# Attention and FFN on one core: weighted sums alternate between two banks, GpSimd's low halves stand ahead of its additions, and the next tile's normalisation and cast move to other engines

## The reference

```python
xn = _layernorm(x)                                    # x: 8 x 1024 x 128
Q = einsum('bnd,hdk->bhnk', xn, proj_q)               # 8 heads
K = einsum('bmd,dk->bmk', xn, proj_k)                 # one key and one value head
V = einsum('bmd,dv->bmv', xn, proj_v)
weights = softmax(einsum('bhnk,bmk->bhnm', Q, K), axis=-1)
O = einsum('bhnm,bmv->bhnv', weights, V)
Y = einsum('bhnv,hdv->bnd', O, proj_o)
mid = einsum('amh,ehn->aemn', xn, w1)                 # 8 experts, no activation
ffn = einsum('aemn,enh->amh', mid, w2)
return x + Y + ffn
```

## Time and profile before

| what | value |
|---|---|
| median of 3 runs | 1693.48 us (1692.24 to 1694.28) |
| profiled execution, its own time | 1692.57 us |
| its span, first to last instruction | 1690.8 us |
| granted TensorE clock, mean | 0.999 |
| busy: PE, PEld | 1655.1 us (98%), 1212.9 us (72%) |
| busy: DVE, ACT, POOL | 1281.2 us (76%), 1294.1 us (77%), 1335.8 us (79%) |
| matmuls, low halves on GpSimd | 18820, 512 |

### The profile page before, as it was taken

One profiled execution on the slowest core, in us unless ns is written; L12 is line 12 of the kernel. 1 busy time (PEld: TensorE's weight loads), 2 busy tenths in 40 slices (PEclk: granted clock), 3 DMA queues, 4 the chain that ended last, 5 costly groups with the idle time before them and its releaser, 6 DMA issues. The chain is left out here.

```text
span 1690.8 us, 46211 instructions
## 1 busy us (share of the span) xinstructions
PE 1655.1 (98%) x18820; PEld 1212.9 (72%) x18820; DVE 1281.2 (76%) x2761; ACT 1294.1 (77%) x1296; POOL 1335.8 (79%) x956
## 2 busy tenths in 40 slices
PE   7999999999999999999999999999999999999997
PEld 6777777777777777777777777777777777777774
DVE  5777777777777777777777777777777777777774
ACT  4777777777777777777777777777777777877874
POOL 2687888788788788878878878887887888788785
PEclk9999999999999999999999999999999999999999
DMA  7000000000000000000000000000000000000000
GB/s 227 2 2 2 2 2 14 2 2 2 8 8 2 1 2 8 8 2 2 2 8 8 2 1 2 8 8 2 2 2 14 2 2 2 2 14 2 2 2 13
DMA packets 16175, 16.71 MB, mean 10 GB/s; under 512 B 416, under 2 KB 12192, under 8 KB 15968
## 3 DMA queue, kind: packets, MB, share of 16 engines
q1 hardware_dynamic: 14928, 13.24, 2.7%
q10 hardware_dynamic: 1040, 0.52, 0.1%
HBM read 9.57 MB, written 4.19 MB: 8 GB/s over the span
## 5 line engine op out<-in xcount | busy, mean ns | idle before, releaser
L281 POOL TENSOR_TENSOR pr_lo<-pr,pr_hi 128x1024 f16<-128x1024 f32 x512 | 1087.7, 2135 | 328.5 <-ACT pr_hi L364 328.5
L357 ACT ACTIVATE pr<-s_ps,boost,scale 128x1024 f32<-128x1024 f32 x512 | 616.9, 1205 | 241.3 <-PE s_ps L514 222.4
L729 DVE TENSOR_REDUCE key_max<-s_ps 128x128 f16<-128x1024 f32 x512 | 625.7, 1222 | 0.1
L364 ACT ACTIVATE pr_hi<-pr 128x1024 f16<-128x1024 f32 x512 | 525.4, 1051 | 8.1
L512 PE MATMUL s_ps<-g_lo,xT 128*128 128x128 f16 x4096 | 512.9, 219 | 2.1 <-DVE g_lo L742 1.0
L514 PE MATMUL s_ps<-g_hi,xT 128*128 128x128 f16 x4096 | 512.3, 219 | 0.0
L512 PEld LDWEIGHTS s_ps<-g_lo,xT 128*128 128x128 f16 x4096 | 399.3, 98 | 41.7 <-DVE g_lo L742 11.1
L514 PEld LDWEIGHTS s_ps<-g_hi,xT 128*128 128x128 f16 x4096 | 400.8, 98 | 29.9
L398 PE MATMUL t_ps<-pr_hi,xn_hi 128*128 128x512 f16 x1024 | 388.3, 379 | 16.9 <-POOL pr_lo L281 3.2
L400 PE MATMUL t_ps<-pr_hi,xn_lo 128*128 128x512 f16 x1024 | 388.4, 379 | 0.0
L399 PE MATMUL t_ps<-pr_lo,xn_hi 128*128 128x512 f16 x1024 | 388.4, 379 | 0.0
(11 more groups left out here) (117 smaller groups left out, 1548.0 us busy)
## 6 DMA issues: line engine op xcount, KB each, us to landing
out_dram<-xacc SPq DMA_DIRECT2D x16, 256.0 KB, 2.3
w_sb<-in_L_ffn_w_dram SPq DMA_DIRECT2D x1, 2048.0 KB, 10.0
pr<-in_L_attn_proj_q_dram ACTq DMA_DIRECT2D x1, 512.0 KB, 4.4
xacc<-in_L_attn_x_dram SPq DMA_DIRECT2D x2, 256.0 KB, 4.9
pr<-in_L_attn_proj_o_dram SPq DMA_DIRECT2D x1, 512.0 KB, 6.3
xacc<-in_L_attn_x_dram SPq DMA_DIRECT2D x1, 128.0 KB, 6.2
wkv<-in_L_attn_proj_k_dram SPq DMA_DIRECT2D x1, 64.0 KB, 2.7
wkv<-in_L_attn_proj_v_dram SPq DMA_DIRECT2D x1, 64.0 KB, 4.2
```

The costliest lines, as they stand in the source:

```text
L281: pool.tensor_tensor(pr_lo[:, u % RING, :], pr32[:, u % PR, :], pr_hi[:, u % RING, :], ALU.subtract)\
L357: act.activation(pr32[:, u % PR, :], both_banks(u), ACT.Exp, bias=boost[:, 0:1], scale=scale[:, 0:1])\
L364: act.activation(pr_hi[:, u % RING, :], pr32[:, u % PR, :], ACT.Copy).then_inc(p_hi_ready, 1)
L729: dve.tensor_reduce(key_max[:, u % 2, :], both_banks(u).rearrange("p (t q) -> p q t", q=P), AX_X, ALU.max).then_inc(keys_max, 1)
```

## The change

- PSUM: `t_ps` is two banks, and block k's sum lies in bank k % 2 (`sum_bank`). `turn_ps` is gone: the transposed maxima and the row lie in the bank that no sum is using; in period 2 of a block the transposed maxima lie in the scores bank of the next high pass's second half.
- The sum's tiles are spread two to a period (before 3, 2, 2, 1), and tile 0 of the next block starts at the end of period 2: its first product before the transpose of the key maxima, the other two behind it.
- In period 3 the row of maxima follows the high products at once, and VectorE writes it before it reduces the keys.
- GpSimd: `p_low` comes first in each period; the additions of heads move back by one period. VectorE subtracts the last unit's low half and does the last addition.
- The next tile's normalisation moves from VectorE to GpSimd, its cast from VectorE to ScalarE, and their places in the pair change.
- `head_out(k, 1)` and `scale_head(k, 1)` go behind the FFN and the transposed tile. The load of x is cut once more, with tiles 10 to 15 ahead of w2.

The diff's pieces stand in this order: PSUM and its helpers; GpSimd; ScalarE's cast; TensorE's `high_pass`, `weigh` and its loop; VectorE's loop and its end.

```diff
-        t_ps = pb("t_ps", [P, BANK])
-        turn_ps = pb("turn_ps", [P, BANK])
+        t_ps = pb("t_ps", [P, 2 * BANK])
...
+        def summing(n):
+            return (n + 1) // 4 - 2
+        def sum_bank(k):
+            return t_ps[:, (k % 2) * BANK:(k % 2 + 1) * BANK]
+        def turn_bank(n):
+            return sum_bank(summing(n) + 1)
+        def maxima_turned(u):
+            if u % 4 == 2:
+                return bank(u + 1, 1)[:, 0:P // 2].bitcast(F16)
+            return turn_bank(u)[:, 0:P // 2].bitcast(F16)
+        def maxima_row(u):
+            return turn_bank(u + 1)[:, 2 * P:3 * P]
...
+            def normalise_next(tile):
+                pool.wait_ge(ln_rstd, tile + 1)
+                pool.wait_ge(ln_hi, tile)
+                pool.wait_ge(xn_ready, tile)
+                pool.tensor_scalar(xn32[:, 0, 1:D], xacc[:, tile, 1:D], mean_var[:, AHEAD, 0:1],
+                                   rstd[:, AHEAD:AHEAD + 1], ALU.subtract, ALU.mult).then_inc(ln_xn32, 1)
...
-                if at == 3 and 0 <= k - 2 < BLOCKS:
-                    add_head(k - 2, 0, ffn_adds)
+                if 1 <= n < UNITS:
+                    p_low(n - 1)
                 if at == 0 and 0 <= k - 3 < BLOCKS:
-                    add_head(k - 3, 1, ffn_adds)
+                    add_head(k - 3, 0, ffn_adds)
...
+                if at == 1 and 0 <= k - 3 < BLOCKS - 1:
+                    add_head(k - 3, 1, ffn_adds)
-                if n % 8 == 7 and (tile := ln_tile(n // 8)) is not None:
+                if n % 8 == 2 and (tile := ln_tile(n // 8)) is not None:
                     pool.wait_ge(ln_var, tile - AHEAD + len(FIRST_TILES) + 1)
...
-                if n % 8 == 4 and (tile := ln_tile(n // 8 - 1)) is not None:
+                if n % 8 == 3 and (tile := ln_tile(n // 8)) is not None:
+                    normalise_next(tile)
+                if n % 8 == 7 and (tile := ln_tile(n // 8)) is not None:
                     xn_low(tile, 0, 1)
-                if 1 <= n <= UNITS:
-                    p_low(n - 1)
...
+                if n % 8 == 6 and (tile := ln_tile(n // 8)) is not None:
+                    split_high(tile, 0, 1)
...
+                    if j == 3:
+                        pe.wait_ge(max_found, u)
...
+                    if t == 0:
+                        pe.wait_ge(p_lo_ready, 4 * k + 4)
+                        if k >= 2:
+                            pe.wait_ge(t_lo_ready, k - 1)
+                        pe.wait_ge(bias_ready, min(4 * k + 6, UNITS))
...
             for n in range(PERIODS):
...
-                chunk(n, 0)
-                if 1 <= n <= UNITS and row_later:
+                if 1 <= n <= UNITS and at == 3:
                     max_to_row(n - 1)
-                chunk(n, 1)
+                chunk(n, 0)
                 small_products(n)
                 if 1 <= n <= UNITS:
                     low_passes(n - 1)
+                if at == 2:
+                    chunk(n, 1, rest=False)
                 if n < UNITS:
                     turn_keys_max(n)
-                chunk(n, 2)
+                chunk(n, 1, first=at != 2)
...
+                if n == UNITS + 1:
+                    p_low_last()
+            last = query_tile(BLOCKS - 1) + 2
+            dve.wait_ge(y_scaled, 2 * BLOCKS)
+            dve.wait_ge(ffn_added, TILES)
+            dve.wait_ge(y_added, 2 * BLOCKS - 4)
+            dve.tensor_tensor(xacc[:, last:last + 2, :], xacc[:, last:last + 2, :], y_tmp[:, 1, :, :], ALU.add)\
+               .then_inc(y_added, 1)
```

More of the change, by code:

```diff
@@ L206, in projected @@
         def projected(k):
-            return bank(4 * (k - 1) + 2, 1) if k >= 1 else t_ps[:, :]
+            return bank(4 * (k - 1) + 2, 1) if k >= 1 else sum_bank(0)
         def head_part(k, g):
@@ L522, in turn_keys_max, with weigh @@
                     pe.wait_ge(bias_ready, u)
-                pe.transpose(turn16[:, 0:P], key_max[:, u % 2, :], ident16[:, :]).then_inc(turned, 1)
+                if u == 7:
+                    pe.wait_ge(f_copied, 1)
+                pe.transpose(maxima_turned(u), key_max[:, u % 2, :], ident16[:, :]).then_inc(turned, 1)
             def max_to_row(u):
                 pe.wait_ge(max_found, u + 1)
-                pe.matmul(turn_ps[:, 2 * P:3 * P], minus_max[:, u % 2, :], ident16[:, :], start=True, stop=True)\
+                if u % 4 == 2 and summing(u) >= 0:
+                    pe.wait_ge(t_lo_ready, summing(u) + 1)
+                pe.matmul(maxima_row(u), minus_max[:, u % 2, :], ident16[:, :], start=True, stop=True)\
                   .then_inc(rowed, 1)
-            def weigh(k, t):
-                if t == 0:
-                    pe.wait_ge(p_lo_ready, 4 * k + 4)
-                    if k == 0:
-                        pe.wait_ge(f_copied, 1)
-                    else:
-                        pe.wait_ge(t_lo_ready, k)
+            def weigh(k, t, first, rest):
                 tile = (batch_tile(k) + t) % KEEP
@@ L540, in weigh @@
                 p_hi, p_lo = pr_hi[:, at:at + 4, t * P:(t + 1) * P], pr_lo[:, at:at + 4, t * P:(t + 1) * P]
-                done = three_pass(t_ps[:, :].rearrange("p (j c) -> p j c", j=4), xn_hi[:, tile, :], xn_lo[:, tile, :],
-                                  p_hi, p_lo, start=t == 0, stop=t == NT - 1)
-                if t == NT - 1:
-                    done.then_inc(pv_done, 1)
+                dst = sum_bank(k).rearrange("p (j c) -> p j c", j=4)
+                if first:
+                    if t == 0:
[3 more added lines that the diff above has]
+                        pe.wait_ge(bias_ready, min(4 * k + 6, UNITS))
+                        if k == 1:
+                            pe.wait_ge(f_copied, 1)
+                    pe.matmul(dst, xn_hi[:, tile, :], p_hi, start=t == 0, stop=False)
+                if rest:
+                    pe.matmul(dst, xn_hi[:, tile, :], p_lo, start=False, stop=False)
+                    done = pe.matmul(dst, xn_lo[:, tile, :], p_hi, start=False, stop=t == NT - 1)
+                    if t == NT - 1:
+                        done.then_inc(pv_done, 1)
             def fold_ffn(e):
@@ L550, in fold_ffn @@
                 for c in range(MC):
-                    last = pe.matmul(t_ps[:, 0:D], w1T[:, e, c * P:(c + 1) * P], w2_sb[:, e, c, :],
+                    last = pe.matmul(sum_bank(-1)[:, 0:D], w1T[:, e, c * P:(c + 1) * P], w2_sb[:, e, c, :],
                                      start=e == 0 and c == 0, stop=e == E - 1 and c == MC - 1)
@@ L554, in fold_ffn, with chunk @@
                     last.then_inc(f_ps, 1)
-            def chunk(n, place):
-                k, tiles = weighed(n)
-                for t in tiles[place]:
-                    if k == -2:
-                        turn_w1(t)
-                    if k == -1:
-                        fold_ffn(t)
-                    if 0 <= k < BLOCKS:
-                        weigh(k, t)
+            def chunk(n, place, first=True, rest=True):
+                k, t = summing(n), 2 * ((n + 1) % 4) + 1 + place
+                if t == NT:
+                    k, t = k + 1, 0
+                if k == -2 and rest:
+                    turn_w1(t)
+                if k == -1 and rest:
+                    fold_ffn(t)
+                if 0 <= k < BLOCKS:
+                    weigh(k, t, first, rest)
             def head_out(k, g):
@@ L614, in _ @@
             for n in range(PERIODS):
-                row_later = n % 4 == 3
+                at = n % 4
                 if n < UNITS:
                     high_pass(n, 0)
-                if 1 <= n <= UNITS and not row_later:
+                if 1 <= n <= UNITS and at != 3:
                     max_to_row(n - 1)
@@ L780, in between_maxima @@
                     copy_turned(n, tile)
+                if at == 0 and 0 <= k - 3 < BLOCKS:
+                    scale_head(k - 3, 1)
                 if at == 1 and k + 1 < BLOCKS:
@@ L839, in _ @@
             for n in range(PERIODS):
-                row_later = n % 4 == 3
-                if 1 <= n <= UNITS and not row_later:
+                if 1 <= n <= UNITS:
                     place_bias(n - 1)
```

70 lines of the change are left out of this document (35 added, 35 removed).

## The result

The changed kernel takes 1669.59 us (median of 4 runs, 1668.54 to 1670.23) against 1693.88 us (4 runs beside it): a ratio of 0.9858, 95% interval 0.9841 to 0.9875. That is faster by 24 us, where 48 were forecast, and it is what rival (a) had described. The profiled execution took 1669.67 us, its span 1667.9 us.

What follows compares the result with a forecast made beforehand. TensorE's instruction stream was taken as the bound, with two stalls and both program ends to win: 34.0 + 10.1 + 1.0 + 3.45 - 1.0 = 47.6 us off 1692.57 gives 1645.0 us, range 1641 to 1660.

Steps and rivals of the forecast that it cites:

- rival (a): GpSimd's low halves become the bound, TensorE's first weighted product waiting every second block: 1650 to 1670 us, chance 0.15.
- N: Time of the next tile's normalisation on GpSimd, taken as 0.35 us between bounds of 0.29 and 0.88.
- rival (d): Slower than before: the normalisation in GpSimd's row takes over 1.33 us; 1702 us at 1.5 us; chance 0.05.
- The chain: GpSimd's row of low halves, addition, power and normalisation: ready at T + 12.03 + N, due at 12.48, room 0.45 us.
- T: Instant in a block's period 2 when the low passes are all issued and the transpose of the key maxima starts.
- Two banks: The next block's sum starts in the other bank without waiting for VectorE's subtraction: 126 x 0.27 = 34.0 us removed.
- the row: Period 3, maxima's row written before the keys' reduction, so low passes no longer wait: 52 x 0.19 = 10.1 us removed.
- the new wait: The high pass's second half waits for unit 2's maximum in the shared scores bank: 0 to 6 us, taken as 1.
- Rival (c): The sum is not freed, as GpSimd's low half comes late at T: 1680 to 1692 us, chance 0.03.
- Cast on ScalarE: The cast delays ScalarE's exponential by about 0.2 us, at most 0.62, before TensorE's small products; no cost taken.
- The start: TensorE's idle time from 50 to 75 us: between 0 and 1.8 us won, taken as 1.0.
- The end: Last low half and last addition on VectorE: 1.45 us earlier restart, 1.6 clock, 0.4 addition; together 3.45 us.

Runs made afterwards that it cites:

- the scalar form: GpSimd's normalisation instruction with both per-partition operands, cut to fewer columns, run additionally in the kernel with the normalisation behind the low halves: 395 ns on one column.
- the version where N is hidden: Against the changed kernel, GpSimd's normalisation moved one step later, behind the low halves and the additions: 1645.3 us, ratio 0.9715.

## Why the prediction was wrong

The step that failed is the size of N in the part on GpSimd: "It has one input from a tensor, so I take 0.35: no stall." N is 0.83 us. The forecast put the range's bounds rightly at 0.29 and 0.88 and the price of the upper one at 23 us; the number of input tensors was the wrong sign to choose by. A row that pointed the other way was the power, 0.55 us on a single column, which the text used only under rival (d). In the groups by line of the kernel before it stands on 4 and on 2 columns too:

```profile
L266 POOL TENSOR_TENSOR rstd<-var_eps,minus_half 128x4 f32<-128x4 f32 x2 | 2.1, 1037 | 6.4 <-DVE var_eps L696 6.4
...
L266 POOL TENSOR_TENSOR rstd<-var_eps,minus_half 128x2 f32<-128x2 f32 x1 | 0.7, 697 | 0.8 <-DVE var_eps L696 0.8
```

From 1 to 4 columns that is 0.16 us a column, (1037 - 552) / 3, and by this estimate a start of 0.39 us: as much as the scalar form took on one column. The rows of the kernel before could not give N, but they gave reason to doubt that it is near a copy's 0.29 us.

Rival (a), at a chance of 0.15, had the mechanism and the place. That its 1668 is so near 1669.6 is in part luck: its N of 0.88 was 0.05 us too high and its room 0.06 us too large, and the two cancel.

- *The chain*: ready at T + 12.03 + N was exact (12.86 with N = 0.83). The room was 0.39 and not 0.45, because the 0.06 us from GpSimd's end to TensorE's start was left out. That is 3 us of the 24.6.
- *Two banks, the row, the new wait*: forecast 34.0 + 10.1 - 1.0 = 43.1 us. In the version where N is hidden, the stalls fall from 45.0 to 0.2 us and the first high product of the last unit comes 43.1 us earlier, of which 0.7 us are there by period 16. The new wait for the maximum cost nothing, where 1.0 had been set against it. The sum of the parts is right, but its terms do not stand alone: the row ahead without the second bank loses 7.7 us, the second bank's wait in the new order is worth 91 us, the old place of the row 82 us.
- *Rival (c)* was given only 0.03 because "GpSimd no longer adds first". The run with the additions first gives back 47 us, so this part carries the gain as much as the banks do.
- *Cast on ScalarE*: forecast nothing. It took 0.30 us and no wait came of it.
- *The start*: forecast 1.0 us won. At period 16 the changed kernel was 0.5 us behind the old one and the version with N hidden 0.7 ahead. The difference is TensorE's clock in the first 24 us, 0.93 in the one execution and 1.00 in the other (last column but two):

```profile
0.00:24.00 24.00, 16.17 (x103) 13.64 (x103) 10.36 (x49) 7.92 (x10) 5.50 (x15) 0.93 0.98 287
```

```profile
0.00:24.00 24.00, 15.55 (x107) 13.34 (x108) 10.70 (x50) 8.67 (x11) 5.49 (x15) 1.00 1.00 289
```

  It makes 1.1 us before the first period. It differs between executions that have the same instructions there, and the mean clock of the whole program differs between executions of one kernel: the changed kernel took 1668.54 us at a mean clock of 1.000 and 1669.5 to 1670.2 us at 0.998. So the changed lines alone do not bring it about; what does stays open. Period 9 also has a new wait of 1.25 us: c_lo on VectorE took 3.08 us, held by GpSimd's low halves (1.28 before the change), while f_lo fell from 2.23 to 0.77.
- *The end*: forecast 3.45 us, measured 4.5. The clock that stays up came as priced (1.6), and VectorE was held as forecast. Counted from the last unit's first high product, TensorE's restart comes 2.3 us earlier, not 1.45: GpSimd's low halves are done 0.7 us sooner than summed, and VectorE needs 1.08 us behind the hold, not 1.28. The last addition gives 0.6, not 0.4.

The error of 24.6 us is 22.9 us of stall and 1.5 at the start (1.0 forecast as won, 0.5 behind at period 16), less 1.0 at the end; the 1.2 us left are not explained.

The Trainium skill, "GPSIMD Engine Reference", section "Engine selection", says that GpSimd is about twice as slow with two inputs and roughly at line rate with one. The trace does not bear out the second half for this form: the one-input form with two steps took 0.83 us on GpSimd and 0.34 us on VectorE, so the first half was the better guide, though it speaks of two inputs. For the one-input copy, 0.29 us, no run here sets VectorE's beside it. The hold of VectorE's normalisation in period 5 fits the Trainium skill, "SBUF — State Buffer", section "Who interferes with whom", by which a `tensor_scalar` can also enter a mode that takes the pair of ports shared with GpSimd. The trace agrees with the hold: 1.65 us beside a low half and 0.34 us beside an idle GpSimd.

## What to carry to other kernels

Before work is moved to an engine with idle time, find the unbroken row of work on that engine that ends in something the bound engine waits for; idle time in front of that row is no cover for what is put inside it. Here the same 0.82 us cost 24 us inside the row and nothing behind it, one step further in the program. Where the price of the moved instruction is unknown and the room is small (0.39 us against bounds of 0.29 and 0.88), put it outside the row rather than choose a value. And a part that wins little or nothing alone may be what another part rests on: here the row ahead of the reduction lost 7.7 us by itself, and its old place cost 82 us in the new order.
